# First group's attention scores on eight TensorE tiles of 64 rows by 32 columns, keys loaded in four parts

## What is computed

```python
h = tok(x)                                    # interpolation, spectrum, soft minimum
h = h + attn(layernorm(h), Wq, Wk, Wv, Wo)    # 8 heads, sigmoid instead of softmax
h = h + ffn(layernorm(h), ...)                # shared MLP and the best 2 of 4 experts

def attn(q_input):                            # b signals, s tokens, f = 64, h = 8
    qkt = einsum('bifh,bjfh->bijh', q, k)
    a = sigmoid(qkt * 8)
    wv = einsum('bijh,bjfh->bifh', a, v)
    return relu(wv.reshape(b * s, f * h) @ Wo)
```

## Time and profile before

| | |
|---|---|
| median of 3 runs | 159.5 us (158.09 to 161.44) |
| the profiled execution | 159.61 us |
| its span, first to last instruction | 157.8 us |
| PE busy | 146.2 us, 93% |
| ACT busy | 119.1 us, 75% |
| DVE busy | 110.8 us, 70% |
| share of the chain that ended last | PE 75%, ACT 7%, DVE 7%, POOL 4%, issue 2% |
| L476, scores of group 0 | 64 matmuls, 27.3 to 37 us |
| L485, scores of groups 1 to 7 | 448 matmuls, 37.5 to 98.8 us |

### The profile page before, as it was taken

One profiled execution on the slowest core, in us unless ns is written; L12 is line 12 of the kernel. 1 busy time (PEld: TensorE's weight loads), 2 busy tenths in 40 slices (PEclk: granted clock), 3 DMA queues, 4 the chain that ended last, 5 costly groups with the idle time before them and its releaser, 6 DMA issues.

```text
span 157.8 us, 6710 instructions
## 1 busy us (share of the span) xinstructions
PE 146.2 (93%) x2856; PEld 87.5 (55%) x2856; DVE 110.8 (70%) x281; ACT 119.1 (75%) x163; POOL 55.3 (35%) x102
## 2 busy tenths in 40 slices
PE   7999686999997999999999999999999999999980
PEld 2478432544574666666665656443657567476480
DVE  2497998998877558586863154879488987877760
ACT  3698982887977899999997989779647867758510
POOL 7000019697695834737356225457000000000000
PEclk9999857999999999999999999999999999999999
DMA  4390000276696692777989700110001011010112
GB/s 118 102 258 1 4 0 0 67 181 145 197 255 206 201 229 72 210 215 224 165 250 179 149 4 13 25 37 0 6 4 32 5 36 34 5 32 13 30 35 67
DMA packets 16722, 15.02 MB, mean 95 GB/s; under 512 B 4780, under 2 KB 15952, under 8 KB 16628
## 3 DMA queue, kind: packets, MB, share of 16 engines
q1 hardware_dynamic: 15924, 13.99, 35.0%
q10 hardware_dynamic: 768, 0.59, 1.3%
HBM read 9.06 MB, written 4.60 MB: 87 GB/s over the span
## 4 chain that ended last, share of the span: by engine, by line
PE 75%; ACT 7%; DVE 7%; POOL 4%; issue 2%; DMA 2%; DVEq 0%; POOLq 0%
PE ps L503 16%; PE ps L485 16%; PE ps L616 9%; PE ps L632 9%; PE ps L514 5%; PE ps L674 4%; PE ps L642 3%; PE ps L696 2%; PE ps L717 2%; DMA area<-x_in 2%; PE ps L540 2%; ACT area L1244 2%; PE ps L444 2%; PE ps L476 1%; ACT square L1242 1%
## 5 line engine op out<-in xcount | busy, mean ns | idle before, releaser
L1309 ACT ACTIVATE probs<-ps 125x1000 f32<-125x1000 f32 x64 | 63.0, 1005 | 8.4 <-PE ps L485 4.1
L503 PE MATMUL ps<-probs,xn 124*32 124x250 f32 (+1 forms) x512 | 40.2, 375 | 0.3 <-ACT probs L1309 0.3
L485 PE MATMUL ps<-YS,XT 128*32 128x500 f16 x448 | 35.9, 375 | 1.0 <-issue 1.0
L1327 ACT ACTIVATE area<-ps,wf 128x500 f32<-128x500 f32 x32 | 21.1, 672 | 7.7 <-PE ps L616 7.7
L936 DVE COPY ZS<-ps 128x250 f32<-128x250 f32 x32 | 13.2, 414 | 17.7 <-PE ps L503 17.7
L503 PEld LDWEIGHTS ps<-probs,xn 124*32 124x32 f32 (+1 forms) x512 | 16.4, 109 | 12.0 <-ACT probs L1309 1.4
L1341 ACT ACTIVATE area<-ps,wf 128x500 f32<-128x500 f32 x20 | 13.5, 676 | 4.7 <-PE ps L642 2.4
L632 PE MATMUL ps<-area,wf 128*64 128x500 f32 x64 | 16.3, 584 | 0.0
L514 PEld LDWEIGHTS ps<-outW,ZS 128*32 128x32 f32 (+1 forms) x512 | 11.7, 108 | 4.8 <-issue 0.9
L485 PEld LDWEIGHTS ps<-YS,XT 128*32 128x32 f16 x448 | 11.2, 96 | 5.6 <-issue 1.7
L514 PE MATMUL ps<-outW,ZS 128*32 128x64 f32 (+1 forms) x512 | 13.1, 219 | 0.2 <-issue 0.2
(11 more groups left out here) (170 smaller groups left out, 260.8 us busy)
## 6 DMA issues: line engine op xcount, KB each, us to landing
YS<-y_stage SPq DMA_DIRECT2D x28, 250.0 KB, 4.1
y_stage<-YP SPq DMA_DIRECT2D x10, 250.0 KB, 3.7
tower_out<-res SPq DMA_DIRECT2D x7, 124.0 KB
wf<-wf_in SPq DMA_DIRECT2D x1, 648.0 KB, 5.8
y_stage<-YP SPq DMA_DIRECT2D x5, 125.0 KB, 3.9
wa<-wa_in SPq DMA_DIRECT2D x1, 512.0 KB, 5.0
y_stage<-YP ACTq DMA_DIRECT2D x3, 125.0 KB, 3.0
ch<-ch_in SPq DMA_DIRECT2D x1, 160.0 KB, 4.8
```

The source lines that it names most:

```text
L485: last = mm(ps[k0:k1, 2 * (n % 2) + j, 0:TG].rearrange("p (h n) -> p h n", h=2), XT[:, g % 3, (2 * bb + cj) * P + k0:(2 * bb + cj) * P + k ...
L503: last = mm(ps[R * hh:R * hh + R, 4 + bb, half * TB:(half + 1) * TB], xn[0:keys, 4 * g + 2 * bb + cj, :], probs[0:keys, n % 3, hh, :], sta ...
L1309: fn(probs[:, n % 3].rearrange("p (j h) n -> p j (h n)", j=2), ps[0:P, 2 * (n % 2):2 * (n % 2) + 2, 0:TG], ACT.Sigmoid, scale=SCORE_SCALE) ...
L1327: fn(H1[:, g % 2, e, :], ps[:, n % 3, 0:TG], ACT.Relu, bias=wf[:, WF["b1"][0] + e:WF["b1"][0] + e + 1]).then_inc(l1_act, 1)
```

## The change

In group 0, each matmul of `scores` is split into four by the key: part `c` loads the keys `32c` to `32c+31` (29 keys in the last) as weights and writes the PSUM partitions of the same numbers. With two heads `j`, that makes eight tiles of 64 rows by 32 columns. A step has 32 matmuls and 32 weight loads instead of 8 and 8, each still with 250 moving columns. `R` is 32, `P` is 125.

```diff
                         for hl in range(2):
-                            for j in range(2):
-                                last = mm(ps[0:P, 2 * (n % 2) + j, i * TB:(i + 1) * TB],
-                                          XT[F * j:F * j + F, 0, key:key + P],
-                                          YS[F * j:F * j + F, 0, 2 * pair + hl, bb * TB:(bb + 1) * TB],
-                                          start=(hl == 0), stop=(hl == 1))
+                            for c in range(4):
+                                k0, k1 = R * c, min(R * c + R, P)
+                                for j in range(2):
+                                    last = mm(ps[k0:k1, 2 * (n % 2) + j, i * TB:(i + 1) * TB],
+                                              XT[F * j:F * j + F, 0, key + k0:key + k1],
+                                              YS[F * j:F * j + F, 0, 2 * pair + hl, bb * TB:(bb + 1) * TB],
+                                              start=(hl == 0), stop=(hl == 1))
                     last.then_inc(s_mm, 1)
                     return
```

## The result

| | before | after |
|---|---|---|
| median of 6 runs | 158.28 us (157.9 to 161.44) | 162.88 us (159.68 to 164.67) |
| the profiled execution | 159.61 us | 162.28 us |
| its span | 157.8 us | 160.5 us |
| after / before | | 1.0159, 95% interval 1.009 to 1.0228 |

The ratio compares the faster executions alone (2 of the 6 of the changed kernel), while the medians take in all and both profiles of the changed kernel are of slower ones, so where its faster ones lose time is in no profile. By the ratio the kernel became 2.5 us slower. So the change costs 0.8 to 1.6% by the two ratios; that it is under 2% is shown by the second interval, not by the first.

What follows compares the result with a forecast made beforehand. PE, 93% busy, was taken as the bound, in group 0 only behind the wait of `scores(4)`. Pace 0.1 plus late block 0.9, other terms 0, made +1.0 us: 160.5, own range 159.8 to 161.5, whole range 158.3 to 162.6.

Steps and rivals of the forecast that it cites:

- What bounds: Group 0: up to the wait of `scores(4)` POOL and DVE bound; behind it PE, three and a half steps.
- Rounds, shape, loads, pace: `scores` of group 0: 0 us each for streaming rounds, shape switch and weight loads; matmul pace adds 0.1 us.
- The block in `scores(7)`: Instruction block beginning in `scores(7)` comes late by 1.15 us, middle of 0 and 2.3; 0.9 us reaches the path.
- The later pauses: Later instruction stalls, 0.15 + 0.98 = 1.13 us, move half a block but keep their sum; ends 0 and twice 1.13.
- Sigmoid 7: Sign in group 0: the sigmoid of n = 7 should start 0.5 to 1 us later than 37.54.
- A: Rival: blocks come in time, or later stalls shrink by what the new one costs; 159.5, chance 0.27.
- B: Rival: the tile-shape switch in group 0 gets cheap; 158.5, or 157.4 with later stalls gone; chance 0.12.
- C: Rival: matmul starts set the pace of `scores`, 25 ns each, +0.46 a step; 162.7, chance 0.06.
- D: Rival: fetch stalls at upper ends, 2.05 at `scores(7)` and 1.13 more later; 162.8, chance 0.10.

Runs made afterwards that it cites:

- the second interval: The changed kernel measured once more, unaltered, against the kernel before: ratio 1.0081 (1.0035 to 1.0128).
- the held read-back: The changed kernel, with SP holding the first read-back of group 1 until `scores(6)` is done: ratio 1.0228 (1.0108 to 1.0348).
- the padded kernels: Short warm-up matmuls add PE instructions ahead of group 0: kernel before, 90, 120, 180 more, 1.0155, 1.0021, 0.9978; changed kernel, 90, 180 more, 0.9962 (again 1.0069), 0.9985.
- The two-part kernels: Group 0's `scores` split in two by key instead of the change's four (64 x 64 tiles), run twice: ratios 0.9957 and 1.0039.
- the kernel with 384 in the warm-up: The kernel before, `scores` unsplit, with 384 more PE instructions, all in the warm-up: ratio 0.9973 (0.992 to 1.0025).
- the same padded kernel: The changed kernel with 90 more PE instructions ahead of group 0, from short warm-up matmuls, measured twice: ratios 0.9962 and 1.0069.

## Why the prediction was right

The direction, the mechanism and its place were right, and the measured 1.0159 on 159.5 is 162.0 us, within the range (158.3 to 162.6), though outside the forecast's own 159.8 to 161.5. The size was low: +1.0 us was said, +2.5 and +1.3 us were measured. The plain median of the six runs, 162.88, lies above the whole range. That 2.5 us still fell inside owes something to luck: the range was wide enough for what was mis-sized below.

*What bounds.* Right. The low part (now at L1056) still ends the wait of `scores(4)`, and the path behind it is PE.

*Rounds, shape, loads, pace.* Right. `scores` 0.55, `mix` 0.56: no streaming gained, the switch as dear as before, no pace of starts down to 0.105 / 8 = 13 ns a matmul. The trace has more than this average: inside a round of eight tiles the matmuls start 3 to 4 ns apart, and then 85 to 95 ns pass before the next round. The 0.1 us that I added for the pace was a small gain instead, 0.02 a step. Weight loads are even denser: PE's load timeline has 18 in the 0.22 us ahead of the pause.

```profile
37.08 0.22 PEld L478 LDWEIGHTS ps<-YS,XT 64*32 64x32 f16 x18 [0.42 <-issue]
```

*The block in `scores(7)`.* Right in place: the 18th matmul of 32 in `scores(7)`, where the sum had the border at its beginning. The term was mis-sized. I took the middle of 0 and 2.3, 1.15; the chain has 1.47, and by the starts of `scores(7)` and `mix(5)` (37.08 and 39.38, against 0.56 normally) PE lost 1.74. It arrived as 1.42, less 0.3 of room as against the 0.24 assumed. From entering the block before to going on PE took 5.2 us (33.86 to 39.05), near the 5.7 of the two late blocks and far from 3.4: the loaded DMA was the case to take, not the middle. The lower end, no pause at 3.4 us, was not reached even with DMA at 0.19: the held read-back took 3.8 there.

*The later pauses.* This step failed. I kept their sum at 1.13 and had left out the 0.21 at 90.89; the profile has 1.63 after and 2.35 in the second one. That they move with the instruction count was right, as was that each can go either way, as the padded kernels show. But the padded kernels had 0.2 to 1.3 in all, so the new places of the changed kernel are bad ones, above all number 3009, a `mix` at about 80 us, with 1.06 us in both profiles. The two-part kernels have 256 instructions fewer up to there, and pause at the same place of the program (number 2753) for 0.79 and 1.06 us; the kernel with 384 in the warm-up does not. Why a place is bad in most profiles but not in all stays open; that the traffic of the other queues repeats is only argued.

*Sigmoid 7* was to start 0.5 to 1 later; against the restart of `scores(4)` it is 5.98 instead of 4.87, so 1.1 later.

*Rivals.* A (nothing arrives) is what the padded kernels did, not this one. B was refuted by the 0.56 of `mix`, C by the 0.55 of `scores`. D, with 2.05 here and 2.26 later (1.13 more than before), is nearer to the second profile (1.41 here and 2.35 later) than the forecast is; its 0.10 was too little beside the forecast's 0.45. C's 25 ns from start to start is not in the trace, which has 3 to 4.

## What to carry to other kernels

Where PE runs without a break and DMA is busy, the number of instructions is a cost of its own: count the instructions between two pauses of "issue" (those of the sequencer too), and if it is a multiple of 256, a loaded block was probably late; the end of the packet on the instruction queue, 1.2 to 1.7 us ahead of the restart, confirms it. A split that streams the same columns in more instructions has nothing to gain and uses up its blocks faster. An edit far from any slow place can move the borders of blocks and shift the time by about 1%, so look for these pauses before a small difference is put down to the edit itself, and pad one variant to see. Adding padding is no lasting cure, since the same padded kernel measured 0.996 and 1.007.

## What the runs showed of the hardware

A pause ends 1.2 to 1.7 us after the end of the packet on the instruction queue: in the changed kernel the packet started at 36.53 and took 1.17, and PE went on at 39.05. In the four pauses of before and the changed kernel over 0.4 us this distance is 1.24 to 1.45. All 38 pauses in the attention stages of the 14 profiles have it (1.16 to 1.67), and none of the other 157 block borders there was crossed sooner than 1.2 us after its packet's end. There the packet starts from 0.3 us before to 4.5 us after PE enters the block before, in the pair above 2.7 with DMA at 0.86 and 1.2 with DMA at 0.19. So PE works in this case as if it held two blocks of 256, the one it works on and the next; that is worked out from these times.

The profile hides part of a pause. The matmuls of `scores` are listed with 0.27 us of latency each, so a gap under that is not idle time in the view: the held read-back's `scores(7)` lost 0.34 us and the view shows no idle time at all. The distance from start to start shows it.

A change of the tile's rows alone, 128 x 32 to 64 x 32 and back, costs 0.13 in `scores` and 0.14 in `mix`, as much as a change of rows and columns. The Trainium skill, "TensorEngine Tiling (Array Packing)", Key Properties, states that changing the tiling mode drains TensorE. This trace agrees for a change of rows alone, in so far as it costs these 0.27 us a step.
